# State-space block and attention on one core: one of four output sums goes from VectorE to GpSimd for 38 of 64 states, idle products fill empty slots, and a softmax is spread over three slots

## Chip, core and metric

One core of one Trainium2 chip. The metric is device microseconds of one launch. Everything is float32.

## What is computed

The reference has three stages, added to `x` (2 batches, 1024 rows, 256 features) one after the other:

- A mask by row norm keeps some rows (`x * keep`).
- A selective state-space block (Mamba), d_inner 512, 16 states: `xz = rmsnorm(x) @ in_proj`, a causal convolution of 4 taps and silu on the first half, `dt, B, C = xi @ x_proj`, `delta = softplus(dt @ dt_w + dt_b)`, then per channel d and state s `h = exp(delta * A[d, s]) * h + delta * xi * B[s]` along time and `y = sum over s of h * C[s]`, then `(y + xi * D) * silu(z) @ out_proj`.
- An attention whose query is the same for all rows of a head, so that with one common mask row all rows of a batch have one output, and a gated feed-forward net on that one row.

The part that the change touches is `y = sum over s of h[:, t, s] * C[t, s]` and the attention of batch 0.

## The kernel before

Time is cut into 4 **chunks** of 512 steps (two per batch; c is the chunk). A **state step** n = 16c + s handles state s of chunk c, so there are 64. Channels are 4 tiles of 128 (m), the 512 time steps are 4 blocks of 128 (i = 0 to 3).

One state step is spread over the engines like this:

- GpSimd (`input_step`, L1353): two products of 128x1024, `delta*x*B[s]`, into slot n % 4 of the ring `hb`. It may write a slot only when all transposes of state n - 4 are done (`hT_ready`). It runs several states ahead.
- ScalarE (`exp_step`, L1217): four times `exp(delta * A)` into the two halves of `dA` (PSUM). The i-th needs the scan of the one two before.
- VectorE (`scan_step`, L1686): four scans of 128x512 along time.
- TensorE (`transposes`, L794): for each time block i, four 128x128 transposes that put time on the partitions, into `hT[:, i % 2]` (PSUM). Block 2 can follow only when block 0 has been read, block 3 only when block 1 has.
- Blocks 0 and 2: ScalarE multiplies by C (`mul_step`, L1227) into `hc`, TensorE adds it up in PSUM over the 16 states (`reduce`, L566).
- Blocks 1 and 3: VectorE multiplies by C and adds to `yTd` in SBUF in one instruction (`mac_step`, L1702; for s = 0 it only multiplies, L1698).

The order on each engine is written out by hand. Every state step has two **slots**, 2n and 2n + 1 (within a chunk: slots 0 to 31, slot 2s and 2s + 1). In step n the scans, exponentials and inputs are those of state n, the rest is that of state n - 1: TensorE does transposes (n-1, 0), (n-1, 1), the jobs of slot 2n, transposes (n-1, 2), (n-1, 3), `reduce` of both blocks, the jobs of slot 2n + 1. VectorE does scans 0 and 1, `mac_step(n-1, 1)`, what it reads of jobs, scans 2 and 3, `mac_step(n-1, 3)`, what it reads of jobs. ScalarE does exp 0 and 1, `mul_step(n-1, 0)`, its reads, exp 2 and 3, `mul_step(n-1, 2)`, `carry_step`, its reads. A job is read by the other engines one slot after TensorE has made it.

Jobs of the loop (`BESIDE`, from the tables `PROLOGUE`, `EPILOGUE`, `LAST_EPILOGUE`, `ATT`) are the next chunk's preparation and the last chunk's end: T and I (slots 3 to 7, norm scaling and projection), V (slots 8, 10, 12, convolutions), X (14), XT and D (18, 20, 21, softplus: three passes on ScalarE and one on VectorE each), Z (22 to 25), Y (slot 1, the finished sums `yTd` of blocks 1 and 3 turned back; in the last chunk slots 1 and 2), O (11, 16), R (28, 30). In the last chunk there is no next one, and the attention of batch 0 (jobs A, G, GT, M, RR, S0, S1, PT, YV, YT, VV, WO) has its slots. A job's output is one of two PSUM banks in turn (`pp`), which it may write when the job two before has been read.

GpSimd has more to do in each chunk for the next one: `row_scaling` at s = 3 (L1372), the four taps of one convolution tile (`conv_taps`, L1386, L1389, L1391) after the inputs of s = 4 and s = 5, of which the first waits until ScalarE has copied job I of tile 1 to `xr` (L1013), `conv_finish` at s = 7 (L1361, L1363), `step_times_input` at s = 13 and 14 (L1403).

`softmax(0)` on VectorE (L1535 to L1541): after S1 it takes the maximum, waits for ScalarE's exponential (L1116) and takes the reciprocal, all in slot 18 of the last chunk.

`keep_warm(k)` (L765) issues k products of the identity with itself, which nobody reads; each is two records in the trace. Before the change they stand in the head and in the tail behind the loop only.

## Time and profile before

| | |
|---|---|
| time, median of 3 runs | 580.53 us (580.28 to 581.11) |
| time of the profiled execution | 581.45 us |
| its span, first to last instruction | 579.3 us |
| loop of 64 state steps, from the span's start | 43.6 to 512.3 us |
| chunk 0, 1, 2, 3 | 123.7, 116.9, 115.1, 113.0 us |
| VectorE busy in chunk 0, 1, 2, 3 | 115.4, 108.3, 104.6, 106.6 us |
| ScalarE busy | 85.1, 82.8, 83.9, 65.7 us |
| GpSimd busy | 98.5, 89.5, 89.1, 63.5 us |
| mean granted TensorE clock | 0.89, 0.96, 0.96, 0.89 |

Times are microseconds from the span's start. PE is TensorE, DVE VectorE, ACT ScalarE, POOL GpSimd. Durations of neighbours on one engine overlap by some hundredths, so what an instruction costs its engine is the distance of two starts. PEclk is the granted TensorE clock, 1.00 for 2.4 GHz and 0.50 for 1.2 GHz. Matmul ends are modelled, so a busy PE is not a PE at its peak.

### The profile page before, as it was taken

How to read it: one execution, taken by the hardware profiler on the slowest of the kernel's cores; microseconds unless marked ns; L12 is line 12 of the kernel's file. 1: busy time of each engine (PE TensorE's matmuls, PEld its weight loads, DVE VectorE, ACT ScalarE, POOL GpSimd, SP SyncE). 2: the span in 40 equal slices, each digit the busy share in tenths (PEclk: the TensorE clock that was granted, in tenths of full speed). 3: DMA queues.
4: the chain of work that ended last, by engine and by line, in shares of the span. 5: the costliest groups of instructions: out<-in, count | busy, mean ns of one | idle time of the engine just before them, and what ended most of it. 6: DMA issues, size and time to landing. Idle time of an engine off the chain costs nothing.

```text
span 579.3 us, 7844 instructions
## 1 busy us (share of the span) xinstructions
PE 481.0 (83%) x2753; PEld 339.3 (59%) x2753; DVE 485.7 (84%) x569; ACT 352.5 (61%) x612; POOL 357.9 (62%) x215
## 2 busy tenths in 40 slices
PE   8968998789668999796689998966897867889992
PEld 6424664465457666554566665545785555878651
DVE  4779989987999899989998999799999989861512
ACT  3765666678765667886757768877466557521210
POOL 5039699747884698777856987787567548100001
PEclk9979999857999999979999999799998879699997
DMA  9331011110111011111110110111111860019004
GB/s 292 101 112 36 37 37 37 39 38 36 37 36 37 36 39 40 36 37 37 38 36 26 48 40 37 37 37 36 38 37 37 294 259 1 1 47 369 13 1 150
DMA packets 17918, 38.87 MB, mean 67 GB/s; under 512 B 1665, under 2 KB 10497, under 8 KB 17874
## 3 DMA queue, kind: packets, MB, share of 16 engines
q1 hardware_dynamic: 17874, 38.32, 19.0%
q8 instruction: 24, 0.39, 0.3%
q14 instruction: 20, 0.16, 0.1%
HBM read 36.08 MB, written 2.23 MB: 66 GB/s over the span
## 4 chain that ended last, share of the span: by engine, by line
PE 36%; DVE 33%; issue 16%; ACT 7%; POOL 6%; DVEq 0%; POOLq 0%; ACTq 0%
DVE scanmem L1686 19%; DVE yTd L1702 8%; PE hT L794 6%; PE pp L508 5%; POOL scanmem L1353 5%; PE pp L532 4%; PE pp L592 3%; PE yacc L566 3%; PE dA L765 2%; PE pp L558 2%; ACT hc L1227 2%; DVE yTd L1611 1%; PE pp L736 1%; PE yacc L562 1%; PE pp L664 1%
## 5 line engine op out<-in xcount | busy, mean ns | idle before, releaser
L1353 POOL TENSOR_TENSOR scanmem<-par,scanmem 128x1024 f32<-128x1024 f32 x128 | 299.1, 2362 | 94.7 <-PE hT L794 59.8
L1217 ACT ACTIVATE dA<-par,Aneg 128x512 f32<-128x512 f32 x256 | 172.5, 690 | 71.3 <-DVE scanmem L1686 70.2
L794 PE MATMUL hT<-con,scanmem 128*128 128x128 f32 x1024 | 158.7, 293 | 60.5 <-DVE yTd L1702 36.8
L794 PEld LDWEIGHTS hT<-con,scanmem 128*128 128x128 f32 x1024 | 122.0, 149 | 118.7 <-DVE yTd L1702 49.0
L1686 DVE TENSOR_TENSOR_SCAN scanmem<-dA,carry,scanmem 128x512 f32<-128x512 f32 x128 | 156.9, 1269 | 2.5 <-ACT dA L1217 2.4
L1686 DVE TENSOR_TENSOR_SCAN scanmem<-dA,scanmem 128x512 f32<-128x512 f32 x128 | 149.2, 1208 | 3.4 <-ACT dA L1217 3.0
L1227 ACT ACTIVATE hc<-hT,CTs 128x512 f32<-128x512 f32 x128 | 87.2, 681 | 78.1 <-PE hT L794 77.6
L1702 DVE SCALAR_TENSOR_TENSOR yTd<-hT,CTs,yTd 128x512 f32<-128x512 f32 x120 | 87.9, 733 | 10.9 <-PE hT L794 10.7
L566 PE MATMUL yacc<-con,hc 128*128 128x128 f32 x512 | 77.1, 293 | 5.8 <-ACT hc L1227 5.8
L566 PEld LDWEIGHTS yacc<-con,hc 128*128 128x128 f32 x512 | 63.2, 151 | 10.0 <-ACT hc L1227 6.5
L508 PE MATMUL pp<-xnT,wi 128*128 128x512 f32 x120 | 63.1, 658 | 5.1 <-ACT xnT L993 3.2
L532 PE MATMUL pp<-xr,diag 128*128 128x512 f32 x88 | 39.4, 592 | 0.0
L508 PEld LDWEIGHTS pp<-xnT,wi 128*128 128x128 f32 x120 | 23.1, 212 | 25.4 <-issue 18.6
L1423 POOL TENSOR_TENSOR par<-xt,hc 128x1024 f32<-128x1024 f32 x1 | 2.4, 2352 | 52.8 <-ACT hc L1269 52.8
L592 PE MATMUL pp<-wo,par 128*128 128x256 f32 x128 | 28.9, 380 | 0.8 <-DVE par L1467 0.8
L592 PEld LDWEIGHTS pp<-wo,par 128*128 128x128 f32 x128 | 23.8, 191 | 4.0 <-DVE par L1467 1.1
L532 PEld LDWEIGHTS pp<-xr,diag 128*128 128x128 f32 x88 | 16.0, 190 | 16.8 <-issue 16.5
L558 PE MATMUL pp<-dbc,wdt 17*128 17x512 f32 x28 | 19.8, 807 | 2.8 <-DVE par L1497 2.8
L1497 DVE SCALAR_TENSOR_TENSOR par<-pp,par 128x512 f32<-128x512 f32 x14 | 9.6, 690 | 13.2 <-ACT par L1088 10.5
L765 PE MATMUL dA<-con 128*128 128x128 f32 x110 | 17.1, 289 | 0.0
L765 PEld LDWEIGHTS dA<-con 128*128 128x128 f32 x110 | 13.9, 192 | 4.7 <-issue 4.6
L1386 POOL TENSOR_SCALAR par<-xr,half_w,half_b 128x512 f32<-128x512 f32 x3 | 2.3, 762 | 23.0 <-ACT xr L1013 23.0
(194 smaller groups left out, 487.8 us busy)
## 6 DMA issues: line engine op xcount, KB each, us to landing
scanmem<-brow SPq DMA_DIRECT2D x32, 512.0 KB, 3.6
par<-in SPq DMA_DIRECT2D x1, 4096.0 KB, 18.1
scanmem<-in SPq DMA_DIRECT2D x1, 4096.0 KB, 15.1
xt<-in SPq DMA_DIRECT2D x4, 512.0 KB, 6.5
wi<-in SPq DMA_DIRECT2D x2, 1024.0 KB, 6.7
out<-par SPq DMA_DIRECT2D x4, 512.0 KB, 4.1
aw<-in SPq DMA_DIRECT2D x5, 256.0 KB, 6.6
xr<-in SPq DMA_DIRECT2D x1, 1024.0 KB, 8.8
```

Of the source, the lines that this page charges most:

```text
L508: last = mm(o, win[:, k, col:col + P], xnT[:, k, :], start=k == 0, stop=k == KD - 1)
L532: last = mm(o, dg[:, m, k, :], xr3[:, m, k:k + T], start=k == 0, stop=k == KC - 1)
L558: return mm(o, wdt[:, m * P:(m + 1) * P], dbc[0:DR + 1, :], start=True, stop=True)
L566: return mm(o[:, m * P:(m + 1) * P], src, ident, start=False, stop=last, is_transpose=True, skip_group_check=True)
L592: last = mm(o[:, i * DM:(i + 1) * DM], dx(e)[:, m, t0:t0 + P], wo[:, m, :], start=m == 0, stop=m == CT - 1)
L765: mm(dst, ident, ident, start=True, stop=True)
L794: last = nc.tensor.transpose(hT[:, i % 2, m * P:(m + 1) * P], hb[:, n % RING, m, i * P:(i + 1) * P], ident)
L1217: A(dA[:, m % 2, :], delta(c)[:, m, :], ACT.Exp, scale=Aneg[:, m * NS + s:m * NS + s + 1]).then_inc(da_ready, 1)
L1227: A(hc[:, e % 2, :], hT[:, 0, :], ACT.Copy, scale=CTs[:, c % 2, i, s:s + 1]).then_inc(mul_done, 1)
L1353: nc.gpsimd.tensor_tensor(hb[:, n % RING, ms, :], dx(c)[:, ms, :], Bb[:, row:row + 1, :].to_broadcast([P, 2, T]), ALU.mult).then_inc(bx_re ...
L1686: V.tensor_tensor_scan(hb[:, n % RING, m, :], dA[:, m % 2, :], hb[:, n % RING, m, :], start, ALU.mult, ALU.add).then_inc(scan_done, 1)
L1702: V.scalar_tensor_tensor(dst, src, cs, dst, ALU.mult, ALU.add).then_inc(mac_done, 1)
```

## The change

- `by_pool(n)` says for which states block 3 is no longer summed by VectorE: the odd s in chunks 0 to 2 (24 states) and s = 1 to 14 in chunk 3 (14 states). There `mac_step(n, 3)` returns at once. ScalarE gets `pool_mul_step` behind `mul_step(n, 2)`: it multiplies `hT[:, 1]` by C into one of two buffers in SBUF (`for_pool`). GpSimd gets `add_step(n)`, which adds that buffer to `yTd`. It stands **between the two input products of state n + 4**.
- The sum of block 3 is one chain through both engines: VectorE's `mac_step(n, 3)` of an even s waits for GpSimd's sum of n - 1, and GpSimd's sum waits for VectorE's of n - 1. Job Y of block 3 waits for the chunk's last sum, which is GpSimd's (s = 15) in chunks 0 to 2. Transposes (n, 1) wait for what has last read `hT[:, 1]`: `mac_step(n-1, 3)`, or `pool_mul_step(n-1)`.
- Idle products: 2 or 3 before each job D, A, G, GT, M, RR, PT, YV, YT, VV and WO of the loop (59 in all, `WARM_JOB`), and 6 in an empty even or 4 in an empty odd slot (66 in all: slots 15 to 17 of chunk 0, slots 15 and 17 of chunks 1 and 2, slots 4, 7, 11, 13, 20, 22, 26 of chunk 3).
- In chunk 3 PT, YV, YT and VV move one slot back. The softmax of batch 0 is spread: maximum in slot 18, ScalarE's exponential in slot 19, reciprocal in slot 20.

The diff, without the parts that only name semaphores or repeat a wait's new count:

```diff
-ATT = [6, 8, 8, 10, 12, 14, 15, 16, 17, 20, 22, 23, 24, 27]
+ATT = [6, 8, 8, 10, 12, 14, 15, 16, 17, 21, 23, 24, 25, 27]
...
+def by_pool(n):
+
+    c, s = n // NS, n % NS
+    return 0 < s < NS - 1 if c == NCH - 1 else s % 2 == 1
+
+def pool_sums(n):
+
+    return sum(by_pool(j) for j in range(n + 1))
+
+def vector_sums(n, i):
+
+    return 2 * n + (i + 1) // 2 - pool_sums(n if i == 3 else n - 1)
...
+def idle_slot(h):
+
+    c, at = h // (2 * NS), h % (2 * NS)
+    job = ORDER[INDEX[next_job(h)] - 2]
+    return not BESIDE[h] and SLOT.get(job, -2) <= h - 2 and at in WARM_AT[c == NCH - 1]
...
+WARM_SLOT = {0: 6, 1: 4}
+WARM_AT = {False: range(14, 22), True: range(4, 28)}
+WARM_JOB = {"D": 2, "A": 2, "G": 3, "GT": 3, "M": 2, "RR": 2, "PT": 3, "YV": 2, "YT": 3, "VV": 2, "WO": 3}
+SOFTMAX_AT = 2 * (NCH - 1) * NS + 19
...
+        def for_pool(n):
+            room = xnT if n // NS == NCH - 1 else sm[:, :].rearrange("p (a t) -> p a t", t=T)
+            return room[:, pool_sums(n) % 2, :]
...
             def job_Y(job, o):
 
                 _, e, i = job
-                pe.wait_ge(mac_done, 2 * (NS * (e + 1) - 1) + i // 2 + 1)
+                n = NS * (e + 1) - 1
+                pe.wait_ge(mac_done, vector_sums(n, i))
+                if i == 3 and by_pool(n):
+                    pe.wait_ge(pool_sum_done, pool_sums(n))
...
             def run(job):
                 wait_free(job)
+                if job in SLOT:
+                    keep_warm(WARM_JOB.get(job[0], 0), bank(job)[:, 0:P])
                 jobs[job[0]](job, bank(job)).then_inc(job_full, 1)
...
+                if i % 2 == 0 and e >= 1:
+                    pe.wait_ge(mul_done, e)
+                if i == 3:
+                    pe.wait_ge(mac_done, vector_sums(n, 1))
+                if i == 1 and n:
+                    if by_pool(n - 1):
+                        pe.wait_ge(pool_mul_done, pool_sums(n - 1))
+                    else:
+                        pe.wait_ge(mac_done, vector_sums(n - 1, 3))
...
                     for job in BESIDE[2 * n]:
                         run(job)
+                    if idle_slot(2 * n):
+                        wait_free(next_job(2 * n))
+                        keep_warm(WARM_SLOT[0], bank(next_job(2 * n))[:, 0:P])
...
-                if name == "S1":
-                    softmax(n)
+                if job == ("S1", 1, 0):
+                    softmax(1)
...
+            def pool_mul_step(n):
+
+                c, s = n // NS, n % NS
+                if by_pool(n):
+                    act.wait_ge(hT_ready, NT * n + 4)
+                    if pool_sums(n) > 2:
+                        act.wait_ge(pool_sum_done, pool_sums(n) - 2)
+                    A(for_pool(n), hT[:, 1, :], ACT.Copy, scale=CTs[:, c % 2, 3, s:s + 1]).then_inc(pool_mul_done, 1)
...
                         mul_step(n - 1, 2)
+                        pool_mul_step(n - 1)
                         carry_step(n - 1)
                     for job in to_read(2 * n + 1):
                         read(job)
...
+                    if 2 * n + 1 == SOFTMAX_AT:
+                        softmax(0)
...
+            def add_step(n):
+
+                c = n // NS
+                if by_pool(n):
+                    if by_pool(n - 1):
+                        pool.wait_ge(pool_sum_done, pool_sums(n - 1))
+                    else:
+                        pool.wait_ge(mac_done, vector_sums(n - 1, 3))
+                    pool.wait_ge(pool_mul_done, pool_sums(n))
+                    dst = yTd[:, c % 2, 1, :]
+                    nc.gpsimd.tensor_tensor(dst, dst, for_pool(n), ALU.add).then_inc(pool_sum_done, 1)
...
                     input_step(n, 0)
+                    if n >= RING:
+                        add_step(n - RING)
                     input_step(n, 1)
...
+            for n in range(NCH * NS - RING, NCH * NS):
+                add_step(n)
...
             def mac_step(n, i):
 
                 c, s = n // NS, n % NS
-                e = 2 * n + i // 2
+                if i == 3 and by_pool(n):
+                    return
...
-                    dve.wait_ge(mac_done, e - 1)
+                    if i == 3 and by_pool(n - 1):
+                        dve.wait_ge(pool_sum_done, pool_sums(n - 1))
+                    else:
+                        dve.wait_ge(mac_done, vector_sums(n - 1, i))
...
+                    if 2 * n == SOFTMAX_AT + 1:
+                        softmax_sum(0)
```

## Rows read from the trace of the kernel before

**Rows 1.** The page: busy time of the engines, and the chain that ended last.

```profile
PE 481.0 (83%) x2753; PEld 339.3 (59%) x2753; DVE 485.7 (84%) x569; ACT 352.5 (61%) x612; POOL 357.9 (62%) x215
...
PE 36%; DVE 33%; issue 16%; ACT 7%; POOL 6%; DVEq 0%; POOLq 0%; ACTq 0%
```

**Rows 2.** Timeline, VectorE, chunk 3, s = 11: start us, us, instruction, count.

```profile
482.39 0.73 DVE L1702 SCALAR_TENSOR_TENSOR yTd<-hT,CTs,yTd 128x512 f32<-128x512 f32 x1
483.03 2.45 DVE L1686 TENSOR_TENSOR_SCAN scanmem<-dA,carry,scanmem 128x512 f32<-128x512 f32 x2
```

**Rows 3.** Windows: busy us of each engine in six stretches of the loop.

```profile
core 0: us, PE busy (x) PEld busy (x) DVE busy (x) ACT busy (x) POOL busy (x), PEclk, DMA share, GB/s
123.36:142.44 19.08, 18.15 (x59) 10.63 (x60) 14.52 (x17) 14.92 (x26) 10.84 (x7) 0.61 0.08 28
149.40:167.30 17.90, 9.84 (x70) 7.23 (x68) 17.90 (x20) 12.49 (x22) 13.52 (x7) 1.00 0.18 59
240.66:258.34 17.68, 15.49 (x57) 9.32 (x57) 14.81 (x17) 14.65 (x24) 10.79 (x7) 0.71 0.10 31
413.72:435.28 21.56, 20.29 (x147) 17.14 (x146) 20.17 (x24) 12.11 (x21) 12.88 (x6) 1.00 0.08 25
453.75:462.61 8.86, 8.24 (x42) 5.56 (x43) 7.62 (x9) 4.00 (x8) 4.45 (x3) 0.81 1.03 381
498.41:506.48 8.07, 8.07 (x40) 8.07 (x41) 6.17 (x8) 3.63 (x9) 0.00 (x0) 0.50 0.00 0
```

**Rows 4.** Groups by form: the nearest instructions to those that are added.

```profile
L1227 ACT ACTIVATE hc<-hT,CTs 128x512 f32<-128x512 f32 x128 | 87.2, 681 | 78.1 <-PE hT L794 77.6
...
L1391 POOL TENSOR_TENSOR par<-par 128x512 f32<-128x512 f32 x9 | 11.5, 1273 | 0.8
```

**Rows 5.** The chain in order of time: four idle products (start us, us).

```profile
527.25 0.89 PE dA L765 x8
```

**Rows 6.** Timeline, GpSimd, chunk 1, s = 4 to 7.

```profile
192.57 0.76 POOL L1386 TENSOR_SCALAR par<-xr,half_w,half_b 128x512 f32<-128x512 f32 x1 [9.40 <-ACT xr L1013]
...
195.43 4.67 POOL L1353 TENSOR_TENSOR scanmem<-par,scanmem 128x1024 f32<-128x1024 f32 x2
...
204.23 9.31 POOL L1353 TENSOR_TENSOR scanmem<-par,scanmem 128x1024 f32<-128x1024 f32 x4
```

**Rows 7.** Timeline, VectorE: mac_step(18, 3) and mac_step(20, 3) of chunk 1.

```profile
195.45 0.73 DVE L1702 SCALAR_TENSOR_TENSOR yTd<-hT,CTs,yTd 128x512 f32<-128x512 f32 x1
...
209.69 0.73 DVE L1702 SCALAR_TENSOR_TENSOR yTd<-hT,CTs,yTd 128x512 f32<-128x512 f32 x1
```

**Rows 8.** Timeline, TensorE, the same place: job V, behind transposes (19, 1).

```profile
197.71 3.60 PE L532 MATMUL pp<-xr,diag 128*128 128x512 f32 x8
```

**Rows 9.** Timeline, chunk 0, the same place: GpSimd input(5), VectorE mac_step(2, 3).

```profile
73.69 4.70 POOL L1353 TENSOR_TENSOR scanmem<-par,scanmem 128x1024 f32<-128x1024 f32 x2
...
73.67 0.75 DVE L1702 SCALAR_TENSOR_TENSOR yTd<-hT,CTs,yTd 128x512 f32<-128x512 f32 x1
```

**Rows 10.** Timeline, start of chunk 1: job Y of block 3, GpSimd input(19).

```profile
173.58 1.13 PE L562 MATMUL pp<-par,diagD 128*128 128x128 f32 x8 [0.24 <-DVE yTd L1702]
...
171.50 4.68 POOL L1353 TENSOR_TENSOR scanmem<-par,scanmem 128x1024 f32<-128x1024 f32 x2
```

**Rows 11.** Timeline, ScalarE, chunk 1, s = 10: from mul_step(25, 2) to the next exponentials.

```profile
243.77 0.67 ACT L1227 ACTIVATE hc<-hT,CTs 128x512 f32<-128x512 f32 x1
...
247.97 1.28 ACT L1217 ACTIVATE dA<-par,Aneg 128x512 f32<-128x512 f32 x2
```

**Rows 12.** Timeline, the softmax of batch 0: VectorE, ScalarE, VectorE, GpSimd.

```profile
467.06 1.86 DVE L1537 TENSOR_TENSOR st<-st 128x1 f32<-128x1 f32 x1
...
469.14 1.15 ACT L1116 ACTIVATE sm<-sm,st 128x1024 f32<-128x1024 f32 x1 [3.48 <-DVE st L1539]
...
474.01 1.27 DVE L1686 TENSOR_TENSOR_SCAN scanmem<-dA,carry,scanmem 128x512 f32<-128x512 f32 x1
...
466.56 4.65 POOL L1353 TENSOR_TENSOR scanmem<-par,scanmem 128x1024 f32<-128x1024 f32 x2 [1.21 <-PE hT L794]
```

More of the change, by code:

```diff
@@ L141, with next_job @@
 INDEX = {job: q for q, job in enumerate(ORDER)}
+def by_pool(n):
[5 more added lines that the diff above has]
+    return 2 * n + (i + 1) // 2 - pool_sums(n if i == 3 else n - 1)
+SLOT = {job: h for h, jobs in enumerate(BESIDE) for job in jobs}
+def next_job(h):
+    return next(job for job in [job for jobs in BESIDE[h + 1:] for job in jobs] + TAIL)
+def idle_slot(h):
+    c, at = h // (2 * NS), h % (2 * NS)
+    job = ORDER[INDEX[next_job(h)] - 2]
+    return not BESIDE[h] and SLOT.get(job, -2) <= h - 2 and at in WARM_AT[c == NCH - 1]
 def to_read(h):
@@ L314, in build @@
         hT_ready, mul_done, red_done, mac_done = sem("hT_ready"), sem("mul_done"), sem("red_done"), sem("mac_done")
+        pool_mul_done, pool_sum_done = sem("pool_mul_done"), sem("pool_sum_done")
         carry_done, gated = sem("carry_done"), sem("gated")
@@ L789, in transposes @@
                 e = 2 * n + i // 2
-                if e >= 1:
-                    pe.wait_ge(mac_done if i % 2 else mul_done, e)
+                if i % 2 == 0 and e >= 1:
[7 more added lines that the diff above has]
+                        pe.wait_ge(mac_done, vector_sums(n - 1, 3))
                 for m in range(CT):
@@ L865, in _ @@
                         run(job)
+                    if idle_slot(2 * n + 1):
+                        wait_free(next_job(2 * n + 1))
+                        keep_warm(WARM_SLOT[1], bank(next_job(2 * n + 1))[:, 0:P])
             for i in (1, 3):
@@ L1039, in ev_XT @@
                 if n >= 2:
-                    act.wait_ge(mac_done, 2 * NS * (n - 1))
+                    act.wait_ge(mac_done, vector_sums(NS * (n - 1) - 1, 3))
                 w = XW
@@ L1245, in _ @@
                         pool_conv_tanh(c + 1)
+                    if 2 * n == SOFTMAX_AT:
+                        softmax(0)
                     exp_step(n, 2)
@@ L1254, in _ @@
                         pool_conv_tanh(c + 1)
+                    if 2 * n + 1 == SOFTMAX_AT:
+                        softmax(0)
             n = NCH * NS
@@ L1539, in softmax, with softmax_sum @@
                 V.tensor_scalar(st[:, 1:2], st[:, 0:1], -1.0, None, ALU.mult).then_inc(mx_ready, 1)
+            def softmax_sum(b):
                 dve.wait_ge(p_ready, b + 1)
@@ L1600, in read @@
                     if job[1] == 1:
+                        softmax_sum(1)
                         compare_rows()
@@ L1720, in _ @@
                         read(job)
+                    if 2 * n + 1 == SOFTMAX_AT + 1:
+                        softmax_sum(0)
                     if c == 0:
```

## Prediction

> **What bounds the kernel now.** I read the page first. VectorE is busy 84% and TensorE 83% of the span, and the chain that ended last goes over both, 36% and 33% [rows 1]. Neither is the bound throughout, so the windows decide stage by stage. Where a state step has no job, VectorE runs without a gap: a `mac_step` at 482.39 and the next scan at 483.03 [rows 2], so a sum costs VectorE 0.64 us of its time (0.73 by duration), and a plain step of two such rounds takes 2 x (2.45 + 0.64) less two overlaps of 0.1, some 6.0 us. In chunk 0, from s = 13, it is busy 17.90 of 17.90 us with TensorE at 9.84 [rows 3]. Elsewhere another engine holds: at s = 10 and 11 of chunks 0 and 1 the clock is 0.61 and 0.71 and VectorE is busy 14.52 of 19.08 and 14.81 of 17.68 us; s = 2 to 4 of chunk 3 has TensorE busy 20.29 of 21.56; s = 14 of chunk 3 has it busy all 8.07 us at clock 0.50, the 1.2 GHz level [rows 3]. GpSimd seems free (62%), but what it does is in strict order, and that order has a hole: at s = 4 it stands 9.40 us for job I's copy, then does convolution taps and only at 195.43 the inputs of state 21 [rows 6].
>
> **Sums that leave VectorE.** 38 go, at 0.64 us, 24.3 us of VectorE time. It shortens the kernel only where VectorE ends the step. By the windows I count 16: s = 6, 8, 12, 14 of chunk 0, s = 12, 14 of chunks 1 and 2, s = 5 to 7, 10 to 13 and 15 of chunk 3. That is -10.2 us. The other 22 are in the terms below or behind TensorE (V and O jobs at s = 4 to 8).
>
> **What takes them over.** ScalarE gets 38 multiplications like L1227, 0.68 us each, 25.9 us; GpSimd 38 additions like L1391, 1.27 us each, 48.4 us [rows 4]. ScalarE's lie beside the scans where it has room: in a plain step it does four exponentials (two take 1.28 [rows 11]) and two products, some 3.9 of 6.0 us. The next exponential, queued behind the new product, has to wait for a scan anyhow. It has no room at s = 10 of chunks 1 and 2: from the product at 243.77 it goes through softplus to the exponentials at 247.97 without a gap [rows 11]. There the product costs its 0.61 us of pace, less 0.1. GpSimd would need 4.65 + 1.27 = 5.9 us a step in chunk 3, where VectorE needs 5.4, but it is ahead by up to the ring's four states: the input of state 19 starts at 171.50 [rows 10], before VectorE has begun state 17 behind job Y. That is two states, some 12 us, and 14 steps of 0.5 us eat 7 of them. I take 0; the bound is +3.
>
> **The added waits.** This is the part that speaks against the change. The sum of an even s waits for GpSimd's sum of the state before, and that stands behind the first input of a state four later. At chunk 1: the sum of state 17 can end at 195.43 + 2.34 + 1.27 = 199.04 [rows 4, 6]. VectorE comes to `mac_step(18, 3)` at 195.45 [rows 7]: 3.6 us late. Queued behind it on VectorE are the scans of state 20. On TensorE transposes (19, 1) wait for it, and behind them job V, which started at 197.71 [rows 8]. It would start near 200.8, and TensorE is full from there on, so 3.1 us stay. The next such sum, 19, ends after the input at 208.9 (the third of four from 204.23) plus 2.34 plus two additions, 213.8; VectorE now comes at 209.69 + 3.6 = 213.3 [rows 6, 7]: +0.5. At the chunk's start job Y of block 3 began at 173.58; the sum of state 15 ends at 171.50 + 2.34 + 1.27 = 175.1 [rows 10], 1.5 us late, and transposes (16, 0) stand behind it on TensorE; with the 0.64 that VectorE saves just before, +0.6 stays. Chunk 2 repeats chunk 1: together +8.4. In chunk 0 the sum of state 1 ends at 73.69 + 2.35 + 1.27 = 77.3 against 73.67 [rows 9], 3.6 late too, but VectorE, not TensorE, has slack right behind it; I take half, +1.9 with the sum of state 3. Job Y of chunk 2 gives +0.3. Sum +10.6; the ends are 5 (if TensorE's slack takes more) and 15 (each in full and twice in chunk 0). From s = 6 on GpSimd is early enough. Convolution tile 1 ends 2.5 us later, still before job X.
>
> **Idle products.** Four cost 0.89 us [rows 5], so 0.22 each; 125 are 27.8 us of TensorE. Most lie in idle time. Not covered: s = 7 to 9 of chunks 1 and 2 (10 products, 2.2 us, TensorE nearly full), +0.8 each; s = 2 to 4 of chunk 3, 17 products, 3.7 us against 1.3 us idle [rows 3], less what VectorE saves, +1.3. Together +2.9, ends 0 and 7.
>
> **What the clock gives back.** If the products hold it at 2.4 GHz, each stretch falls to its next bound. Chunk 0, s = 10, 11: 19.08 us with VectorE at 14.5 and ScalarE at 14.9 (15.5 with the new product) [rows 3]; the softplus chain keeps some, so -2.4. Chunks 1 and 2: 17.68 us, -1.8 by the clock and +0.5 by ScalarE, -1.3 each. Chunk 3: s = 8, 8.86 us at 0.81, to 7.4, -1.5; s = 14, 8.07 to 6.1, -2.0 (6.17 of VectorE less 0.64, and the warm products). Sum -8.5; ends 0 and -13. A rule of the skill is weighed here. The row shows: 17.9 us in which TensorE did hardly anything but transposes, busy 9.84, at clock 1.00 [rows 3]. The Trainium skill, "TensorE: Matmul & The Clock Gate", Part 4, says that transposes do not count as busy for the gate in the same way. By it the loop's shorter steps would do nothing for the clock, and only the products would; this trace speaks against it.
>
> **The softmax.** Before, VectorE goes through maximum and wait, and `exp` runs 469.14 to 470.3 with nothing beside it; scan (58, 0) starts at 474.01 [rows 12]. After, ScalarE has done both exponentials before `mx_ready` (near 469.1), VectorE does scans (57, 2) and (57, 3) at once, and (58, 0) starts near 471.5. That is -2.5 with the sum that is gone. The 128x1 `tensor_tensor` took 1.86 us and ended at 468.92, where GpSimd's instruction ended (half of 4.65 from 466.56) [rows 12]; it can cost 0.1 to 2.3 and I leave it. The Trainium skill, "GPSIMD Engine Reference", Key points, says that GpSimd contends with VectorE instructions that have two SBUF inputs: the trace agrees here, and the sums and scans have one input in PSUM.
>
> **Sum.** -10.2 + 10.6 + 2.9 - 8.5 - 2.5 = -7.7 us on the profiled execution's 581.45, so 573.8. The median of the runs lies 0.9 lower: 573.0.
>
> **Rivals.** (a) The waits decide, and the result is slower. The place is `mac_step(18, 3)`, its twin in chunk 2 and state 2: TensorE stands about 3 us, and if the clock falls there, job V (3.60 us at 2.4 GHz) takes twice as long. With waits 15, V +3.6 twice, the products 6 and half of the clock's gain: -10.2 + 15 + 7.2 + 6 - 4.2 - 2.5 = +11, 592; a middle case gives 584. It decides once waits and products exceed 21. For it: the 3.6 us are read off two rows each. Against it: the jobs around are dense at clock 1.00. 0.18.
> (b) The waits hardly bite, because GpSimd's hole moves earlier too or TensorE's backlog hides them: waits 2, clock -11, so -18.8, 562. Against it: the hole ends with ScalarE's copy, which no part of the change makes earlier. 0.13.
> (c) The change doesn't do what it says: the idle products do not hold the clock. D jobs have 17 rows, and the fall at s = 10 comes while they run. Then -7.7 + 8.5, 582 less 0.9, within the measurement. 0.13.
> My forecast, 567 to 579: 0.56.
>
> **Range and chances.** 565 to 583: (a)'s outer half and (b)'s fall out. A measurement tells 0.2%, about 1.2 us, from no change. Faster: 0.56 + 0.13 + a little of (c) = 0.72. Same 0.08. Slower 0.20.
>
> **What would show it.** Plain steps of chunk 3 at 5.4 us instead of 6.0; a gap of some 3 us on VectorE ahead of the sum of state 18 and 34, ended by GpSimd's addition, with TensorE idle ahead of V; chunks 1 and 2 longer than 116.9 and 115.1, chunk 3 near 104; clock 1.00 at s = 10 and 11. I am wrong if VectorE has no such gap, if the clock still falls at s = 10, or if chunk 3 does not become shorter by 7 or more.

## Result: slower, 593.7 us

The median of the changed kernel is 593.69 us (588.76 to 596.3, 4 runs) against 580.40 us of the kernel before (578.6 to 581.11, 4 runs): ratio 1.0225, 95% interval 1.0178 to 1.0272. The profiled execution took 595.01 us with a span of 593.2, 13.9 more than the span before. The forecast of 573.0 was wrong, and so was its range; the number is near that of rival (a)'s full case, 592.

### The profile after

The page of the changed kernel: busy time, the chain that ended last, and the two groups of sums that the change gave to GpSimd.

```profile
PE 500.2 (84%) x3003; PEld 364.6 (61%) x3003; DVE 461.3 (78%) x531; ACT 374.3 (63%) x650; POOL 404.3 (68%) x253
...
PE 49%; DVE 20%; issue 12%; ACT 9%; POOL 9%; DVEq 0%; ACTq 0%; POOLq 0%
...
L1438 POOL TENSOR_TENSOR yTd<-yTd,sm 128x512 f32<-128x512 f32 x24 | 30.5, 1272 | 0.0
...
L1438 POOL TENSOR_TENSOR yTd<-yTd,xnT 128x512 f32<-128x512 f32 x14 | 17.7, 1266 | 9.0 <-ACT xnT L1293 9.0
```

VectorE got rid of 24.4 us, as the instructions that left it say, but fell from 84 to 78% of a longer span. In the chain its share fell from 33 to 20%, TensorE's rose from 36 to 49% and GpSimd's from 6 to 9% [rows 1]. GpSimd's 38 sums took 48.2 us.

Windows of the changed kernel: the four chunks, then the six stretches of [rows 3], in the order s = 10 and 11 of chunk 0, s = 10 and 11 of chunk 1, s = 2 to 4, s = 8 and s = 14 of chunk 3, and s = 13 to 15 of chunk 0.

```profile
core 0: us, PE busy (x) PEld busy (x) DVE busy (x) ACT busy (x) POOL busy (x), PEclk, DMA share, GB/s
44.78:169.38 124.60, 103.87 (x547) 69.90 (x545) 110.78 (x125) 89.18 (x156) 105.49 (x60) 0.93 0.10 35
169.38:295.86 126.48, 105.35 (x590) 74.58 (x588) 103.06 (x109) 87.53 (x142) 100.57 (x58) 0.95 0.11 37
295.86:419.19 123.33, 105.39 (x590) 75.15 (x588) 99.08 (x108) 88.79 (x156) 98.04 (x58) 0.94 0.10 33
419.19:526.36 107.17, 95.44 (x760) 85.22 (x759) 98.06 (x103) 73.64 (x124) 82.76 (x43) 0.97 0.26 95
126.08:145.79 19.71, 17.08 (x71) 10.51 (x71) 13.78 (x17) 15.51 (x27) 12.07 (x8) 0.80 0.08 27
252.22:271.03 18.81, 15.50 (x64) 9.21 (x65) 14.27 (x17) 15.35 (x25) 11.72 (x8) 0.82 0.09 28
432.95:456.87 23.92, 23.92 (x187) 22.03 (x186) 18.40 (x21) 12.82 (x23) 15.62 (x8) 1.00 0.06 24
473.38:480.42 7.04, 6.30 (x41) 4.93 (x42) 6.83 (x10) 4.62 (x9) 6.87 (x4) 1.00 0.92 300
514.37:520.52 6.15, 6.15 (x55) 5.88 (x55) 5.45 (x7) 4.71 (x10) 1.19 (x2) 1.00 0.00 0
152.09:169.38 17.29, 10.30 (x76) 7.85 (x74) 17.29 (x20) 13.33 (x24) 15.14 (x9) 1.00 0.08 30
```

Against 123.7, 116.9, 115.1 and 113.0 us before, the chunks changed by +0.9, +9.6, +8.2 and -5.9; the head before the loop is 1.1 longer, the tail 0.1 shorter. So the loss lies in chunks 1 and 2. Taken step by step (a state step goes from its first scan to the next one's first), it sits in few places, chunk 1 first and chunk 2 second: s = 1 +4.4 and +3.1, s = 3 +3.1 and +3.2, s = 4 +1.2 and +1.2, s = 9 +0.9 and +0.9, s = 2 +0.6 and +0.6, s = 10 +0.7 and +1.2. At s = 10 and 11 the clock rose from 0.61 to 0.80 (chunk 0) and from 0.71 to 0.82 (chunk 1), and yet neither stretch is shorter.

Timeline of the changed kernel at the place of [rows 6, 7, 8], chunk 1: GpSimd, then VectorE's `mac_step(18, 3)`, then TensorE's transposes (19, 1) and job V.

```profile
198.32 0.76 POOL L1469 TENSOR_SCALAR par<-xr,half_w,half_b 128x512 f32<-128x512 f32 x1 [9.39 <-ACT xr L1070]
...
201.18 2.35 POOL L1424 TENSOR_TENSOR scanmem<-par,scanmem 128x1024 f32<-128x1024 f32 x1
...
203.48 1.27 POOL L1438 TENSOR_TENSOR yTd<-yTd,sm 128x512 f32<-128x512 f32 x1
...
204.86 0.75 DVE L1796 SCALAR_TENSOR_TENSOR yTd<-hT,CTs,yTd 128x512 f32<-128x512 f32 x1 [3.34 <-POOL yTd L1438]
...
205.66 1.11 PE L845 MATMUL hT<-con,scanmem 128*128 128x128 f32 x4 [2.48 <-DVE yTd L1796]
...
206.57 4.83 PE L572 MATMUL pp<-xr,diag 128*128 128x512 f32 x8
```

The gap is where the prediction put it and as long: 3.34 us, ended by GpSimd's addition, behind GpSimd's 9.4 us for ScalarE's copy. Behind it job V takes 4.83 us in place of 3.60 [rows 8]: the granted clock, 1.00 before the gap, is 0.50 when the engine starts again. The waits of the same kernel count three such gaps on VectorE, one in each of chunks 0 to 2 (10.3 us in total, 3 times, the longest 3.5):

```profile
DVE yTd L1796 <- POOL yTd L1438: 10.3, 3, 3.5
```

Timeline of the changed kernel at the start of chunk 1, the place of [rows 10]: GpSimd from input(17), TensorE's job Y of block 3, and the first sum of the new chunk on VectorE.

```profile
163.12 2.36 POOL L1424 TENSOR_TENSOR scanmem<-par,scanmem 128x1024 f32<-128x1024 f32 x1 [2.15 <-ACT carry L1299]
165.43 1.27 POOL L1438 TENSOR_TENSOR yTd<-yTd,sm 128x512 f32<-128x512 f32 x1
166.66 6.98 POOL L1424 TENSOR_TENSOR scanmem<-par,scanmem 128x1024 f32<-128x1024 f32 x3
173.62 1.41 POOL L1455 TENSOR_SCALAR par<-con,scl 128x128 f32<-128x128 f32 x4
175.00 2.34 POOL L1424 TENSOR_TENSOR scanmem<-par,scanmem 128x1024 f32<-128x1024 f32 x1
177.30 1.26 POOL L1438 TENSOR_TENSOR yTd<-yTd,sm 128x512 f32<-128x512 f32 x1
...
178.71 2.05 PE L602 MATMUL pp<-par,diagD 128*128 128x128 f32 x8 [3.33 <-POOL yTd L1438]
...
182.64 0.75 DVE L1789 TENSOR_SCALAR yTd<-hT,CTs 128x512 f32<-128x512 f32 x1 [4.26 <-PE hT L845]
```

This gap, which the prediction had at 0.6 us, is as long as the other: TensorE stands 3.33 us, then job Y runs at half clock (2.05 us against 1.13), and VectorE stands 4.26 us. Its twin at the start of chunk 2 is shorter, and there the clock falls only 0.9 us after the restart:

```profile
303.69 1.21 PE L602 MATMUL pp<-par,diagD 128*128 128x128 f32 x8 [1.95 <-POOL yTd L1438]
```

### The profile page after: what moved, and what is told of

Its sections match the earlier page's. It is cut to its first block, busy times and chain, and to the rows that moved or that the text cites. A ratio compares the mean times of both kernels' runs of the same rounds, so it can differ in the third digit from the quotient of the medians.

```text
span 593.2 us, 8393 instructions
## 1 busy us (share of the span) xinstructions
PE 500.2 (84%) x3003; PEld 364.6 (61%) x3003; DVE 461.3 (78%) x531; ACT 374.3 (63%) x650; POOL 404.3 (68%) x253
## 4 chain that ended last, share of the span: by engine, by line
PE 49%; DVE 20%; issue 12%; ACT 9%; POOL 9%; DVEq 0%; ACTq 0%; POOLq 0%
PE hT L845 11%; DVE scanmem L1776 10%; POOL scanmem L1424 6%; PE pp L635 5%; PE pp L572 5%; PE pp L548 4%; PE yacc L606 4%; DVE yTd L1796 4%; PE pp L808 3%; PE dA L808 2%; PE pp L598 2%; POOL yTd L1438 2%; PE pp L584 2%; ACT hc L1284 1%; DVE yTd L1701 1%
## 5 line engine op out<-in xcount | busy, mean ns | idle before, releaser
L845 PE MATMUL hT<-con,scanmem 128*128 128x128 f32 x1024 | 153.5, 289 | 49.7 <-DVE yTd L1796 31.6
L1796 DVE SCALAR_TENSOR_TENSOR yTd<-hT,CTs,yTd 128x512 f32<-128x512 f32 x82 | 60.0, 731 | 17.9 <-POOL yTd L1438 10.3
L606 PE MATMUL yacc<-con,hc 128*128 128x128 f32 x512 | 72.6, 280 | 0.7 <-ACT hc L1284 0.7
L606 PEld LDWEIGHTS yacc<-con,hc 128*128 128x128 f32 x512 | 59.2, 144 | 5.1 <-ACT hc L1284 0.9
L808 PE MATMUL pp<-con 128*128 128x128 f32 x250 | 37.7, 291 | 8.0 <-DVE par L1584 8.0
L572 PE MATMUL pp<-xr,diag 128*128 128x512 f32 x88 | 42.4, 628 | 0.0
L808 PEld LDWEIGHTS pp<-con 128*128 128x128 f32 x250 | 33.1, 203 | 11.9 <-DVE par L1584 10.5
L1438 POOL TENSOR_TENSOR yTd<-yTd,sm 128x512 f32<-128x512 f32 x24 | 30.5, 1272 | 0.0
L1438 POOL TENSOR_TENSOR yTd<-yTd,xnT 128x512 f32<-128x512 f32 x14 | 17.7, 1266 | 9.0 <-ACT xnT L1293 9.0
```

Of the source, the lines that this page charges most:

```text
L572: last = mm(o, dg[:, m, k, :], xr3[:, m, k:k + T], start=k == 0, stop=k == KC - 1)
L606: return mm(o[:, m * P:(m + 1) * P], src, ident, start=False, stop=last, is_transpose=True, skip_group_check=True)
L808: mm(dst, ident, ident, start=True, stop=True)
L845: last = nc.tensor.transpose(hT[:, i % 2, m * P:(m + 1) * P], hb[:, n % RING, m, i * P:(i + 1) * P], ident)
L1438: nc.gpsimd.tensor_tensor(dst, dst, for_pool(n), ALU.add).then_inc(pool_sum_done, 1)
L1796: V.scalar_tensor_tensor(dst, src, cs, dst, ALU.mult, ALU.add).then_inc(mac_done, 1)
```

## The experiments

Two switches of the changed kernel cut the time into parts: which sums GpSimd takes, and which idle products stand. The softmax is spread in all of the runs. Ratios are against the kernel before, run on the same chip. The chip isn't the same in all experiments, so runs of different experiments are best compared by their ratios; a hundredth of a ratio is 5.8 us.

### No sums on GpSimd

```diff
-    return 0 < s < NS - 1 if c == NCH - 1 else s % 2 == 1
+    return False
```

> No state's sum goes to GpSimd; idle products and the spread softmax stay. Theory W (the waits between VectorE's and GpSimd's sums cost about 19 us at the starts of chunks 0 to 2, the saved sums give back about 7): 581 to 584 us, no gap on TensorE ahead of job Y or V. Rival P (the 125 idle products on a full TensorE are the cost): it stays at 589 us or more.

Measured: 582.35 us, ratio 1.0038 (1.0006 to 1.007). The gaps are gone. The products with the softmax alone gain nothing and rather cost.

### No idle products in the loop

```diff
-WARM_AT = {False: range(14, 22), True: range(4, 28)}
-WARM_JOB = {"D": 2, "A": 2, "G": 3, "GT": 3, "M": 2, "RR": 2, "PT": 3, "YV": 2, "YT": 3, "VV": 2, "WO": 3}
+WARM_AT = {False: range(0), True: range(0)}
+WARM_JOB = {}
```

> All idle products of the loop are taken out, the sums on GpSimd and the spread softmax stay. W: the gaps of about 3 us ahead of job Y and job V are still there in chunks 1 and 2, clock low at more places, 588 to 596 us. P: below 582 us.

Measured: 585.15 us, ratio 1.0062 (1.002 to 1.0105), below what the theory of the waits expected and above its rival's bound. The gaps stand: s = 3 of chunk 1 takes 9.48 us, of chunk 2 9.38. But the products cost some 9 us of the changed kernel, where I had them gain. In chunks 1 and 2 job V of this run is at clock 1.00, which the windows of steps s = 1 and of s = 3 and 4 of chunk 1 show:

```profile
172.94:185.25 12.31, 9.52 (x58) 9.02 (x59) 7.32 (x10) 3.79 (x6) 7.90 (x5) 0.72 0.14 44
194.10:211.40 17.30, 14.81 (x77) 9.54 (x76) 12.20 (x12) 11.06 (x19) 14.59 (x11) 1.00 0.10 32
```

The two steps s = 3 and 4 (the second row) took 14.59 us before, 17.30 here, and 18.94 at clock 0.91 in the changed kernel, which has no product at this place either. So the gap costs 2.7 us alone and 4.3 with the clock. The twin of job Y's gap says the same: in chunk 2 the clock did not fall behind it in this run, and s = 1 takes 8.76 us, against 10.09 in the changed kernel and 6.97 before.

### Sums on GpSimd in the last chunk alone

```diff
-    return 0 < s < NS - 1 if c == NCH - 1 else s % 2 == 1
+    return 0 < s < NS - 1 if c == NCH - 1 else False
```

> GpSimd sums only in the last chunk (14 states), where no VectorE sum stands between its own; products and softmax as in the change. W: chunks 1 and 2 back to about 118 and 116 us, chunk 3 stays near 107: 574 to 579 us. P: 589 us or more.

Measured: 573.66 us, ratio 0.9886 (0.9856 to 0.9915), just below the expected range. The 24 sums of chunks 0 to 2 are the whole loss: without them the change is a gain.

### Sums of chunks 0 to 2 only where no gap was: s = 5, 7, 9, 11, 13

```diff
-    return 0 < s < NS - 1 if c == NCH - 1 else s % 2 == 1
+    return 0 < s < NS - 1 if c == NCH - 1 else s in (5, 7, 9, 11, 13)
```

> In chunks 0 to 2 GpSimd leaves states 1, 3 and 15, the ones whose sum comes late, to VectorE and keeps 5, 7, 9, 11, 13 (29 states in all). W: no gap ahead of Y and V, and some saved sums are kept: 571 to 577 us, 1 to 4 below the kernel with GpSimd in the last chunk alone. P: 589 or more. If the sums of s = 5 to 13 also wait, it is above that kernel.

Measured: 576.70 us, ratio 0.9916 (0.9894 to 0.9939). 17 us come back by dropping s = 1, 3 and 15 (18 by the ratios), but it stays 3 us above the run with no sums in these chunks, where I had expected a gain. At s = 10 of chunk 1 the step takes 9.32 us (8.12 with no sums there). Timeline, ScalarE, of this run there, and the new product at the same place in the changed kernel:

```profile
244.29 0.67 ACT L1284 ACTIVATE hc<-hT,CTs 128x512 f32<-128x512 f32 x1
245.48 0.69 ACT L1293 ACTIVATE sm<-hT,CTs 128x512 f32<-128x512 f32 x1 [0.52 <-PE hT L845]
246.06 0.59 ACT L1123 ACTIVATE par<-pp 128x512 f32<-128x512 f32 x1
...
249.69 1.29 ACT L1274 ACTIVATE dA<-par,Aneg 128x512 f32<-128x512 f32 x2
```

```profile
256.06 0.69 ACT L1293 ACTIVATE sm<-hT,CTs 128x512 f32<-128x512 f32 x1
```

The new product waits 0.52 us for transposes of block 3 that no one on ScalarE had to wait for before, and softplus and exponentials stand behind both: 1.2 us on the step, not 0.5. The wait goes with TensorE's clock. In the changed kernel the clock is still 1.00 at this place, the product waits 0.06 us, and the step is 0.74 longer than before. Of the twelve such products at s = 10 of chunks 1 and 2 in the six kernels that have them, ten came while the clock was at 0.50 and waited 0.43 to 0.53 us, and the two at 1.00 waited 0.06. So 0.74 is the product's price and some 0.46 is the clock's.

The product of state 5 costs as well, where the prediction took nothing: s = 6 of chunks 1 and 2 takes 9.77 us in place of 9.20. There it stands on ScalarE ahead of the reading of job V's output, for which VectorE waits 2.47 us in this run and 0.74 before.

### The spread softmax alone

No sums on GpSimd and no products, by the two edits above.

> Only the softmax of batch 0 is spread over three slots and PT to VV stand a slot later; no sums on GpSimd, no idle products. The step at s = 9 of chunk 3 went from 11.4 to 9.4 us in every kernel that has it: 578 to 579 us, 1.5 to 2.5 below the kernel before, chunks 0 to 2 as before. Rival: the gain there came from the clock or from the sums, then 580 to 581.

Measured: 576.25 us, ratio 0.9939 (0.9903 to 0.9975), more of a gain than expected. The softmax's own step, s = 9 of chunk 3, takes 9.45 us in place of 11.40. The rest has another place: s = 14 of chunk 3 takes 6.02 us at clock 1.00, in place of 8.07 at 0.50 [rows 3]. Window of this run there:

```profile
496.62:502.64 6.02, 5.58 (x50) 4.46 (x48) 6.02 (x8) 4.24 (x9) 0.00 (x0) 1.00 0.01 3
```

All thirteen kernels with the spread softmax, whose jobs PT to VV stand one slot later, have clock 1.00 at this step; only the kernel before has 0.50.

### Products only in chunk 0 and in the second part of chunk 3

Over the last-chunk kernel:

```diff
-    return not BESIDE[h] and SLOT.get(job, -2) <= h - 2 and at in WARM_AT[c == NCH - 1]
+    return not BESIDE[h] and SLOT.get(job, -2) <= h - 2 and at in WARM_AT[c == NCH - 1] and (h < 32 or h > 104)
...
-                    keep_warm(WARM_JOB.get(job[0], 0), bank(job)[:, 0:P])
+                    keep_warm(WARM_JOB.get(job[0], 0) if SLOT[job] < 32 or SLOT[job] > 104 else 0, bank(job)[:, 0:P])
```

> GpSimd sums in the last chunk only, idle products in chunk 0 and from slot 10 on of chunk 3, none in chunks 1 and 2 and none at s = 2 to 4 of chunk 3. If products pay only where the clock had been low and TensorE has room: s = 2 to 4 of chunk 3 take 20.5 us instead of 23.0, the rest stays, 569 to 573 us, the fastest. If the products of slots 4 to 8 kept the clock up for later steps: 574 or more.

Measured: 568.70 us, ratio 0.9805 (0.9746 to 0.9864), a little below the expected range. Chunk 3 takes 104.46 us in place of 106.79.

### GpSimd's sums in an array of their own

In chunks 0 to 2 GpSimd takes the odd states but 15 and adds them into its own array (one buffer is left for the products), VectorE adds the others into `yTd`; job Y of block 3 turns both back, with four more transposes. The core of the diff:

```diff
-                    dst = yTd[:, c % 2, 1, :]
+                    dst = yTd[:, c % 2, 1, :] if c == NCH - 1 else sm[:, T:2 * T]
...
-                        dve.wait_ge(pool_sum_done, pool_sums(n - 1))
+                        if c == NCH - 1:
+                            dve.wait_ge(pool_sum_done, pool_sums(n - 1))
+                        else:
+                            dve.wait_ge(mac_done, vector_sums(n - 2, 3))
```

> GpSimd adds its odd states of chunks 0 to 2 into an array of its own, which job Y adds at the end, so that neither engine waits for the other's sum; states 15, 31, 47 stay with VectorE (35 sums on GpSimd, same work otherwise). W (the shared chain is what costs): no gap at s = 1, 3 of the chunks, chunks 1 and 2 near 119 and 117 us, 574 to 579 us. Rival G (GpSimd's and ScalarE's added work itself, wherever its sum goes): 586 us or more.

Measured: 577.17 us, ratio 0.9965 (0.9932 to 0.9997). Timeline of this run at the place of the 3.34 us gap: GpSimd comes out of its 9.39 us as before, and VectorE's sums (L1810) don't wait.

```profile
191.92 0.76 POOL L1480 TENSOR_SCALAR par<-xr,half_w,half_b 128x512 f32<-128x512 f32 x1 [9.39 <-ACT xr L1073]
192.03 0.73 DVE L1810 SCALAR_TENSOR_TENSOR yTd<-hT,CTs,yTd 128x512 f32<-128x512 f32 x1
...
195.03 0.73 DVE L1810 SCALAR_TENSOR_TENSOR yTd<-hT,CTs,yTd 128x512 f32<-128x512 f32 x1
...
198.04 0.73 DVE L1810 SCALAR_TENSOR_TENSOR yTd<-hT,CTs,yTd 128x512 f32<-128x512 f32 x1
```

Step s = 3 takes 6.02 us in place of 9.47. GpSimd does nearly as many sums here (21 in chunks 0 to 2), so what costs is the one chain that goes through both engines, not the work. The closest pair is this run and the one below in which state 15 stays with VectorE: the same 35 sums on GpSimd, once with and once without the shared chain, 1.0165 against 0.9965, 11.6 us. By the ratios it stays 4.6 us above the run with no sums in these chunks; s = 10 of chunk 1 is 9.32 us here too, so ScalarE's part is in it. The four more transposes don't show: s = 1 takes 7.21 and 6.97 us as before.

### No products at the D jobs

Over the last-chunk kernel, `WARM_JOB` without its entry for D.

> As the kernel with GpSimd in the last chunk alone, without the two products ahead of each D job (24 fewer). If these hold TensorE up at s = 9 (8.6 us against 7.7): s = 9 of chunks 1 and 2 back to 7.7, and s = 10, 11 longer by as much if they had kept the clock: 573 to 577. If they only cost: 571 to 572.

Measured: 575.22 us, ratio 0.9934 (0.9902 to 0.9967). Inconclusive: s = 9 of chunks 1 and 2 takes 7.94 and 8.04 us in place of 8.59 and 8.68, most of the way to the 7.7 expected. The median lies where it was expected if these products had kept the clock up, but the steps don't bear that out: s = 10 and 11 take 17.70 us in place of 16.72 in chunk 1, and 15.50 in place of 16.79 in chunk 2. In its profiled execution the tail behind the loop is 3.1 us longer, at a lower clock.

### State 15 stays with VectorE in chunks 0 to 2; states 1 and 3 stay with it

Two kernels, each an edit of the changed one:

```diff
-    return 0 < s < NS - 1 if c == NCH - 1 else s % 2 == 1
+    return 0 < s < NS - 1 and (c == NCH - 1 or s % 2 == 1)
```

> The change, but VectorE keeps the sums of states 15, 31, 47 (35 on GpSimd). W: the gap ahead of job Y is gone (s = 1 of chunks 1 and 2 back to 7.2 and 7.0 from 11.6 and 10.1), the one at s = 3 stays (9.4 us): 584 to 588 us. If the sums of states 1 and 3 alone cause both gaps, no difference from 593.7.

```diff
-    return 0 < s < NS - 1 if c == NCH - 1 else s % 2 == 1
+    return 0 < s < NS - 1 if c == NCH - 1 else s % 2 == 1 and s > 3
```

> The change, but VectorE keeps states 1 and 3 of chunks 0 to 2 (32 on GpSimd). W: s = 3 back to 6.4 and 6.2 us and s = 4 to 8.2 and 8.4, chunk 0 shorter by 3, s = 1 still with job Y's gap (the sum of state 13 is still ahead of that of 15): 582 to 587 us. The two gains together give the kernel with all five kept (576.7).

Measured: 588.72 us, ratio 1.0165 (1.0091 to 1.024), and 584.41, ratio 1.0076 (1.0046 to 1.0107); the first is just above its expected range. The first takes away the gap at job Y (s = 1 of chunk 1 is 7.21 us again) and leaves those at s = 3 (9.48), the second the other way round (11.58 and 6.37). So 5.0 and 9.3 us by the medians, 3.5 and 8.6 by the ratios; dropping both, as above, gives 17.0 or 17.9, more than their sum. The runs of each of these two kernels lie 7 us apart, so this remainder can't be told from their scatter. The steps of the profiled executions do add up: 5.5 us for the first (s = 0 and 1 of chunks 1 to 3, less the 0.66 each that s = 0 had gained) and 11.1 for the second (s = 2 to 6 of chunks 0 to 2), together 16.6.

### Last chunk alone, and no products

> GpSimd sums in the last chunk alone and the spread softmax, no idle products in the loop. Against the kernel with chosen products (568.7) it tells what those in chunk 0 and in the later half of chunk 3 are worth: chunk 0 122.6 to 123.7 instead of 121.3 us, chunk 3 about 104.5 as the steps are ended by VectorE there: 570 to 573 us. If the products of chunk 3 are needed, 574 or more.

Measured: 567.16 us, ratio 0.976 (0.9703 to 0.9818), below what was expected: the products that were left had cost as well. Windows of this run: chunk 0, chunk 3, s = 10 and 11 of chunk 0, s = 2 to 4, 10 and 14 of chunk 3.

```profile
44.84:165.26 120.42, 96.38 (x503) 63.44 (x501) 115.34 (x132) 84.87 (x149) 98.50 (x53) 0.95 0.11 40
396.66:499.65 102.99, 83.29 (x618) 69.77 (x617) 98.77 (x104) 73.12 (x123) 80.56 (x42) 0.95 0.25 94
124.86:140.36 15.50, 12.98 (x59) 7.99 (x58) 14.21 (x18) 14.69 (x26) 10.51 (x7) 0.89 0.11 34
411.09:431.84 20.75, 19.56 (x144) 16.84 (x143) 18.37 (x21) 12.87 (x23) 14.61 (x8) 1.00 0.08 26
464.79:470.37 5.58, 4.66 (x24) 4.00 (x24) 5.50 (x7) 4.96 (x9) 2.28 (x2) 0.60 0.94 385
488.38:493.81 5.43, 5.17 (x48) 4.51 (x48) 5.43 (x6) 4.67 (x9) 0.91 (x2) 1.00 0.00 0
```

The same three stretches of chunk 3 with the products in (windows of the run with the last chunk's sums and all products):

```profile
412.13:435.18 23.05, 23.05 (x182) 21.27 (x181) 18.39 (x22) 12.83 (x23) 14.75 (x8) 1.00 0.07 25
468.06:475.50 7.44, 7.30 (x42) 7.18 (x42) 5.54 (x8) 4.94 (x9) 2.40 (x2) 0.63 0.73 296
492.50:498.66 6.16, 6.16 (x56) 5.89 (x55) 5.45 (x7) 4.71 (x10) 1.10 (x2) 1.00 0.00 0
```

With them TensorE is busy all of the first and the third stretch and sets their length; without them it isn't, at the same clock, and they are 2.3 and 0.7 us shorter. In the second, s = 10, the clock is low either way (0.63 and 0.60), and the products make it 1.9 us longer. A part comes back in the step behind it: with the products s = 11 takes 5.51 us at clock 1.00, without them 6.53 at 0.56. Of the two steps together 0.8 us is left as the products' cost.

### The last chunk, and states 11 and 13 of the others

Over that kernel, a version meant to beat it:

```diff
-    return 0 < s < NS - 1 if c == NCH - 1 else False
+    return 0 < s < NS - 1 if c == NCH - 1 else s in (11, 13)
```

> The last chunk's sums on GpSimd, no idle products, and of chunks 0 to 2 only the sums of states 11 and 13. In the full change those two sums shortened the steps behind them by 0.66 and 0.64 us in chunk 0, 0.66 and 0.38 in chunk 1, 0.66 and 0.16 in chunk 2, in all 3.2 us, with no gap behind them, and the gaps stood at the sums of states 1, 3 and 15. Theory 'the shared sum is worth its time where VectorE ends the step and GpSimd is in time': about 3 us less than the kernel with the last chunk's sums alone (567.2), so near 564, ratio 0.970 to 0.976; steps 12 of chunks 0 to 2 at 6.3 to 6.6 us, and no gap at job Y. Rival 'GpSimd's order hurts wherever it has the chunk's own work too' (the sum of state 13 stands ahead of the row scaling and the inputs at the next chunk's start): 567 to 571, with a gap on TensorE or VectorE in steps 0 to 2 of the next chunk.

Measured: 563.71 us (562.09 to 565.4), ratio 0.9735 (0.9707 to 0.9762), the lowest of all. Windows: s = 12 and s = 14 of chunk 0, of this run and then of the one with the last chunk alone.

```profile
142.03:148.34 6.31, 6.03 (x32) 3.78 (x31) 6.31 (x8) 5.76 (x11) 6.31 (x4) 1.00 0.00 0
154.72:159.85 5.13, 2.98 (x22) 2.13 (x20) 5.13 (x6) 4.20 (x8) 2.99 (x3) 1.00 0.14 47
```

```profile
140.36:147.33 6.97, 6.68 (x38) 4.35 (x36) 6.97 (x10) 5.65 (x11) 6.97 (x4) 1.00 0.00 0
153.70:159.48 5.78, 3.49 (x26) 2.55 (x24) 5.78 (x7) 4.16 (x8) 4.10 (x2) 1.00 0.01 3
```

Both steps are some 0.65 us shorter, all of it VectorE's busy time, and there is no gap at job Y. In chunks 1 and 2 s = 12 gains the same and s = 14 gains 0.40 and 0.17, so the six sums gain 3.2 us by the steps. The whole time can't confirm that: it is 3.45 lower by the medians, which are of two chips, and 1.5 by the ratios, whose intervals overlap.

## Why the prediction was wrong

The ratios above, times the 580.5 us of before, cut the 13.1 us of the result into parts, three of them by more than one pair of runs:

| part | forecast | measured | from |
|---|---|---|---|
| softmax spread | -2.5 | -3.5 | softmax alone |
| 14 sums of the last chunk | -5.1 | -8.8, -10.4 | with products, without |
| 24 sums of chunks 0 to 2 | +5.5 | +19.7, +17.5 | with products, without |
| idle products, clock included | -5.6 | +5.7, +7.3, +9.5 | no sums, last chunk's, all |

(The forecast's 16 steps are split as it counted them, 8 in chunks 0 to 2 and 8 in the last, and -8.5 of the clock stands with +2.9 of the products.) The intervals of these ratios reach 1.7 to 3.4 us to either side, so a difference of two is good to 2.5 to 4 us.

The lengths of the steps in the profiled executions bear out a part of this. Chunks 0 to 2 lose 20.6 us by their 24 sums with the products and 15.8 without, and the loop of 64 steps loses 9.2 us by the products with all sums and 5.8 with the last chunk's. The rest they don't bear out. With no sums the loop is 1.3 us shorter with the products than without. The 14 sums shorten chunk 3 by 1.9 us with the products and by 6.5 without; with the products 5.1 more of the difference stand behind the loop, where the run without sums had a lower clock. Why that tail was slower is open.

**The added waits: the step that failed first.** The sum of +10.6 measured +19.3, by the lengths of steps s = 1 to 4 against before: chunk 0 +1.95 (forecast 1.9), chunk 1 +9.3, chunk 2 +8.1 (4.2 each). ScalarE's part at s = 2, told below, is in it with 1.4. The +0.3 for job Y of chunk 2 came to nothing: s = 1 of chunk 3 is 7.21 us before and after.
- `mac_step(18, 3)` was right: the wait is 3.34 us and step s = 3 is 3.10 longer (forecast 3.1), its twin 3.23. That GpSimd's order has a hole in front of it, and that TensorE stands behind it, is what the rows show.
- "TensorE is full from there on, so 3.1 us stay" left out what the gap does to the clock. Job V costs 4.83 - 3.60 = 1.2 us more in chunk 1 and 5.30 - 3.60 = 1.7 in chunk 2, and the step s = 4 grows by 1.2 in both. Rival (a) had this mechanism, at three times the size.
- "The next such sum, 19" came to nothing: no wait is there. By the time VectorE gets there GpSimd is in time.
- Job Y was sized at +0.6 and cost 4.4 and 3.1. I took GpSimd's times from the kernel before and delayed only the sum itself. Two more delays stand ahead of it: the sum of state 13, which sits between the inputs of state 17 (1.2 us), and `carry_step`, for which input(17) waits and which now stands on ScalarE behind the new product. It ran 3.57 us after the first scan of s = 14 (159.35 against 155.78), now 4.31 (162.78 against 158.47). Of these 2.0 us only 0.8 reached the sum of state 15: input(19) began 15.72 us behind that scan before (171.50) and 16.53 now (175.00), since GpSimd had stood 1.14 us idle ahead of an input in between and no longer does. Against the same mark VectorE's two saved sums made job Y ready 1.3 earlier. With the 1.5 that was forecast this makes 3.6 us of waiting, and 3.33 were measured. The rest of the cost is again the clock: job Y at 2.05 us, not 1.13. The run that keeps state 15 on VectorE has no gap there.

**Sums that leave VectorE.** The rate was right: where VectorE ends the step, each is worth 0.64 us (6.34 to 5.69, 5.77 to 5.13). The count was wrong both ways. In the changed kernel s = 6 and 8 of chunk 0 gained 0.02 and 0.36, while s = 0 of chunks 1 to 3, which the forecast left out, gained 0.66 each. In the last chunk the ratios give 8.8 and 10.4 us for the 14 sums. That this is about 14 times 0.64 proves no count: of the 6.5 us by which chunk 3 is shorter in the pair without products, 1.7 lie at s = 8, where the clock was 0.81 in one run and 1.00 in the other. At equal clocks this step differs by 0.5, which leaves 5.3, near the 5.1 forecast.

**What takes them over.** GpSimd was in time in chunk 3, as taken: 9.0 us of idle ahead of its sums there, for ScalarE's product. ScalarE was not beside other work everywhere. In the runs in which GpSimd sums state 1, s = 2 of chunks 1 and 2 is 0.57 us longer each, and 0.88 in one place. State 5's product costs 0.57 at s = 6. At s = 10 the cost is 0.74 at full clock and 1.2 at half (forecast 0.5), and chunk 0, which the forecast took as free of it, has it too: 8.84 and 8.93 us in the two runs at clock 0.99 and 1.00 with the sum of state 9, against 8.10 to 8.35 in those at 1.00 without.

**Idle products and what the clock gives back: the step that failed as much.** I read off [rows 3] that the clock was low at s = 10, 11 and at s = 8 and 14 of chunk 3, and gave the products credit for 8.5 us. What the runs show:
- At s = 14 of chunk 3 the clock is 1.00 without any product in the loop (5.43 us, row above), and the step is shorter than with them. With the softmax alone it is 1.00 too. The 2.0 us came with the spread softmax and its moved jobs, in all thirteen kernels that have them. That the moved jobs are the reason is likely but not shown: no run moves them without the rest of that part.
- At s = 8 of chunk 3 the execution decided. Seven kernels have the same sums and the same products there, and in five the clock is 1.00 and the step 7.04 us, in two 0.80 and 8.73.
- s = 10 and 11 of chunk 0 have the same instructions in the kernel before and in the run with the last chunk alone and no products: 19.08 us at clock 0.61 [rows 3] and 15.50 at 0.89. The stretch differs as much between two executions as I had credited to the change.
- At s = 11 of chunk 1 the clock is low with products and without (0.70 in the changed kernel, 0.78 with the last chunk's sums and no products).

That is rival (c), which I had as "no gain"; but products in a step that TensorE ends are a cost too, and my +2.9 for it (ends 0 and 7) was near its upper end or past it: s = 2 to 4 of chunk 3 +2.3 (forecast 1.3), s = 10 +1.9 less the 1.0 that s = 11 gets back, s = 14 +0.7, s = 9 of chunks 1 and 2 +0.9 each (0.8 for three steps).

The Trainium skill, "TensorE: Matmul & The Clock Gate", Part 4, says that transposes don't count as busy for the gate in the same way. It was weighed because by it only the products could hold the clock. The stretch of this loop in which TensorE does nothing but transposes, s = 13 to 15 of chunk 0 (last row of the windows above), has clock 1.00 throughout in ten of the fourteen kernels, and in four it falls for a part of it (those with the last chunk's sums and all products, with states 1, 3 and 15 kept, with the softmax alone, and with no products at D). So the rule is not borne out as it stands, and the measurement decides.

**The softmax** went as worked out, its step being 1.95 us shorter by itself and 2.07 with the sum that is gone (forecast 2.5). The other 2.05 of what the softmax alone gained is the clock at s = 14. Timeline of the changed kernel, VectorE's 128x1 instruction, ScalarE's exponential, GpSimd, and VectorE's scans:

```profile
485.11 2.15 DVE L1624 TENSOR_TENSOR st<-st 128x1 f32<-128x1 f32 x1
...
487.48 1.15 ACT L1173 ACTIVATE sm<-sm,st 128x1024 f32<-128x1024 f32 x1 [1.37 <-DVE st L1626]
...
482.56 4.69 POOL L1424 TENSOR_TENSOR scanmem<-par,scanmem 128x1024 f32<-128x1024 f32 x2
...
487.38 4.81 DVE L1776 TENSOR_TENSOR_SCAN scanmem<-dA,carry,scanmem 128x512 f32<-128x512 f32 x4
```

VectorE now goes on with scans at 487.38 while ScalarE's exponential runs, and s = 9 fell from 11.40 to 9.33 us. The 128x1 instruction took 2.15 us (1.86 in [rows 12]) and again ended, at 487.26, where GpSimd's running instruction ended: 482.56 + 4.69 = 487.25 us. The change left that where it was.

**The chances.** The tests named in the text came out as: plain steps of chunk 3 5.4 us, right at s = 6 and 7 (5.38 and 5.44, the others 5.5 to 5.8); the gap of 3 us, right; TensorE idle ahead of V, right; chunks 1 and 2 longer, right, but by 9.6 and 8.2 us where the forecast's own terms make some 2.4 each; chunk 3 near 104, wrong (107.2, so shorter by 5.9 and not by 7 or more); clock 1.00 at s = 10 and 11, wrong (0.80 and 0.82). Two of the three signs of being wrong came up. Rival (a) was the mechanism of the waits; its 0.18 took the clock's fall behind a gap for unlikely, because the jobs around were dense at clock 1.00. Its sum reached +11 with V's clock overpriced (7.2 for 2.5), job Y underpriced, and half of the clock's gain still credited, so that its number came near by luck.

## What to carry to other kernels

When one running sum is shared by two in-order engines, every one of its steps ties the two queues together: follow the slower queue through all it does, from several steps ahead, and move only those terms where the engine that gives ends the step and the one that takes is ahead; here the fastest kernel keeps 20 of the 38, and the other 18, with the idle products, turned a gain of 15 us into a loss of 13. Credit for a higher clock must come from a pair of runs, not from low stretches of one execution, and idle products belong at most where the engine has idle time: here the kernel without them was faster at a lower mean clock. A gap on TensorE costs its length, and often half clock for the work behind it: here in eight of the twelve gaps of 1.95 us and more.
